# A message-passing and hash-expert kernel: 7,424 of its 8,192 edges sorted on the chip into runs of one source and one destination block

## What is computed

```
feat = concatenate([n_f[edge_src], n_f[edge_dst]], axis=1)   # 8192 edges
e_hh = relu(feat[:128]    @ W_hh + b_hh)     # edge tile 0
e_oo = relu(feat[128:768] @ W_oo + b_oo)     # edge tiles 1 to 5
e_ho = relu(feat[768:]    @ W_ho + b_ho)     # edge tiles 6 to 63: the "ho" edges
logit = ([e_hh, e_oo, e_ho] @ W_a + b_a)[:, 0]
ex    = exp(logit - segment_max(logit, edge_dst)[edge_dst])
alpha = ex / segment_sum(ex, edge_dst)[edge_dst]
z_f   = segment_sum(alpha[:, None] * n_f[edge_src], edge_dst)
h_new, o_new = relu([n_f, z_f][:64] @ W_hn + b_hn), relu([n_f, z_f][64:] @ W_on + b_on)
```

## Time and profile before

| | us |
|---|---|
| median of 3 runs | 871.84 (870.72 to 873.1) |
| the profiled execution's own time | 873.71 |
| its span, first to last instruction | 872.1 |
| TensorE busy | 807.4 (93%) |
| VectorE busy | 553.9 (64%) |
| ScalarE busy | 380.8 (44%) |
| GpSimd busy | 122.9 (14%) |

### The profile page before, as it was taken

One profiled execution on the slowest core, in us unless ns is written; L12 is line 12 of the kernel. 1 busy time (PEld: TensorE's weight loads), 2 busy tenths in 40 slices (PEclk: granted clock), 3 DMA queues, 4 the chain that ended last, 5 costly groups with the idle time before them and its releaser, 6 DMA issues.

```text
span 872.1 us, 10861 instructions
## 1 busy us (share of the span) xinstructions
PE 807.4 (93%) x3565; PEld 648.3 (74%) x3566; DVE 553.9 (64%) x822; ACT 380.8 (44%) x512; POOL 122.9 (14%) x143
## 2 busy tenths in 40 slices
PE   4899999979999969569997899999999999999998
PEld 4677788758888857457784578888888888888886
DVE  6874565559998899997645674445555544554443
ACT  3673454337665628154242343333444443344330
POOL 3010010012221336990003200000000000000000
PEclk9899999989999988888897989999999999999999
DMA  8676325312322220302255055555544554445521
GB/s 302 233 285 242 124 49 228 145 38 48 61 48 55 54 97 1 128 1 97 96 193 194 0 193 192 192 192 192 167 159 165 183 186 165 162 168 185 192 97 48
DMA packets 49600, 121.18 MB, mean 139 GB/s; under 512 B 2613, under 2 KB 35765, under 8 KB 47018
## 3 DMA queue, kind: packets, MB, share of 16 engines
q1 hardware_dynamic: 46122, 112.39, 36.0%
q0 software_dynamic: 2976, 8.13, 4.3%
q10 hardware_dynamic: 480, 0.36, 0.2%
HBM read 119.82 MB, written 1.05 MB: 139 GB/s over the span
## 4 chain that ended last, share of the span: by engine, by line
PE 84%; DVE 9%; issue 5%; ACT 1%; DMA 1%; DVEq 1%; POOL 0%; SPq 0%; ACTq 0%
PE ps L1013 19%; PE ps L1015 19%; PE ps L1014 19%; PE ps L1035 13%; PE ps L1042 5%; PE ps L1202 4%; PE ps L983 2%; DVE junk L850 2%; PE ps L1240 1%; PE ps L1257 1%; PE ps L1004 1%; DVE route L938 1%; DVE wlo L674 1%; DMA xt<-in_x_dram 1%; DVE oh_dst L872 1%
## 5 line engine op out<-in xcount | busy, mean ns | idle before, releaser
L674 DVE TENSOR_TENSOR wlo<-raw,whi 128x2048 fp32r<-128x2048 f32 x95 | 215.0, 2288 | 84.9 <-ACT whi L468 84.9
L468 ACT ACTIVATE whi<-raw 128x2048 fp32r<-128x2048 f32 x104 | 195.7, 1910 | 114.9 <-PE ps L1015 99.3
L1013 PE MATMUL ps<-whi,nT_hi 128*128 128x512 f32 x432 | 175.9, 407 | 1.7 <-POOL wlo L413 1.7
L1014 PE MATMUL ps<-whi,nT_lo 128*128 128x512 f32 x432 | 173.2, 401 | 0.0
L1015 PE MATMUL ps<-wlo,nT_hi 128*128 128x512 f32 x432 | 173.0, 400 | 0.0
L1035 PE MATMUL ps<-tab_hi,onehot 128*128 128x512 f32 x252 | 101.1, 401 | 12.3 <-issue 6.4
L1035 PE MATMUL ps<-tab_lo,onehot 128*128 128x512 f32 x252 | 100.3, 398 | 0.0
L1013 PEld LDWEIGHTS ps<-whi,nT_hi 128*128 128x128 f32 x432 | 82.6, 191 | 23.1 <-POOL wlo L413 2.1
L1015 PEld LDWEIGHTS ps<-wlo,nT_hi 128*128 128x128 f32 x432 | 82.8, 192 | 20.3
L1014 PEld LDWEIGHTS ps<-whi,nT_lo 128*128 128x128 f32 x432 | 82.9, 192 | 19.2
L946 DVE TENSOR_TENSOR gw<-act_g,route 128x512 f32<-128x512 f32 x32 | 20.7, 688 | 119.1 <-ACT act_g L635 119.1
(11 more groups left out here) (169 smaller groups left out, 988.1 us busy)
## 6 DMA issues: line engine op xcount, KB each, us to landing
raw<-n_L_ffn_values_down_dram SPq DMA_DIRECT2D x16, 2048.0 KB, 8.3
raw<-in_L_ffn_values_up_dram SPq DMA_DIRECT2D x16, 2048.0 KB, 7.5
raw<-in_L_gnn_W_hh_dram SPq DMA_DIRECT2D x4, 2048.0 KB, 10.2
raw<-in_L_gnn_W_oo_dram SPq DMA_DIRECT2D x4, 2048.0 KB, 7.8
raw<-in_L_gnn_W_ho_dram SPq DMA_DIRECT2D x4, 2048.0 KB, 7.8
raw<-in_L_gnn_W_hn_dram SPq DMA_DIRECT2D x4, 2048.0 KB, 7.4
raw<-in_L_gnn_W_on_dram SPq DMA_DIRECT2D x4, 2048.0 KB, 7.4
idx_b<-in_src_dram POOLq DMA_DIRECT2D x31, 128.0 KB, 3.2
```

The source lines that it names most:

```text
L468: nc.scalar.activation(half(whi, s, j, down), half(raw, s, j, down), ACT.Copy)\
L674: nc.vector.tensor_tensor(half(wlo, s, j, down), half(raw, s, j, down), half(whi, s, j, down).bitcast(F32), ALU.subtract)\
L1013: nc.tensor.matmul(o, a_hi, b_hi, start=start, stop=False)
L1014: nc.tensor.matmul(o, a_lo, b_hi, start=False, stop=False)
```

## The change

The first six tiles (`HEAD`) stay as tiles. The 58 ho tiles are sorted. VectorE computes for every ho edge its bucket, 4 x destination block + source block, one of 16. TensorE counts and ranks the edges (`count_buckets`, `rank_edges`), VectorE turns ranks into slots (`places`), each bucket padded to a multiple of 128, and lists each window's two blocks (`window_rows`). A window is 128 slots of one bucket; 58 tiles and at most 16 paddings make 74 windows, always. The node numbers are moved to their slots by 58 one-hot matmuls, in 15 chunks of up to four (`permute`), whose rows GpSimd and whose columns VectorE makes (`chunk_row`, `chunk_columns`); the matmuls stand among those of the head tiles and of `project(2, 0)`. `decode` copies the result.

Both tables are now stacked by block. TensorE spreads the indices of two windows over the partitions (`spread`, four matmuls of 128 x 128), ScalarE makes the one-hots from them in two instructions of 512 columns (`ring`), and a window takes four matmuls of 128 x 512, whose table blocks come from two registers read with `value_load`. A head tile takes 16 matmuls as before; VectorE makes its eight one-hots. VectorE's `dot` writes into PSUM; `window_peak` updates 64 columns of `segmax` at a place read with a `value_load`. GpSimd makes three tiles of 64 columns per window ahead of that (`same`, `oh_src`, `pen`). The maximum pass has 80 columns instead of 64, with the `lo` work of units 14 and 15 in it, which GpSimd did. In the sums, a window takes one `value_load` and two matmuls of 64 x 64; `oh_dst` is made for 18 or 19 windows at a time. The loops over windows are unrolled, and three pairs of PSUM banks take windows in turn. Nothing in the experts' part changes.

```diff
+HEAD = 6
+FIRST_TILE = [0, 1, HEAD]
+JT = ET - HEAD
+NBK = 16
+WN = JT + NBK
+COLS = HEAD + WN
+CHUNK = 4
+CHUNKS = (JT + CHUNK - 1) // CHUNK
...
+            pool.wait_ge(sorted_ready, 1)
+            for n in range(CHUNKS):
+                if n >= 2:
+                    pool.wait_ge(permuted, n - 1)
+                for j in range(CHUNK * n, min(CHUNK * n + CHUNK, JT)):
+                    last = nc.gpsimd.tensor_scalar(chunk_row[:, n % 2, j % CHUNK, :], iota16[:, 0:P], keep[:, 3, j:j + 1],
+                                                   None, ALU.is_equal)
+                last.then_inc(row_ready, 1)
+
...
+            pool.wait_ge(decoded, 1)
+            pool.wait_ge(gathered, HEAD)
+            for w in range(WN):
+                nc.gpsimd.tensor_scalar(same[:, w % 2, :], iota16[:, 1:NH + 1], slot_idx[:, 1, w:w + 1], None,
+                                        ALU.is_equal).then_inc(win_same, 1)
+                nc.gpsimd.tensor_scalar(oh_src[:, w, :], iota16[:, 1:NH + 1], slot_idx[:, 0, w:w + 1], None,
+                                        ALU.is_equal).then_inc(win_src, 1)
+                pool.wait_ge(win_same, w + 1)
+                nc.gpsimd.tensor_scalar(pen[:, w, :], same[:, w % 2, :], 1.0, -NEVER,
+                                        ALU.subtract, ALU.mult).then_inc(win_pen, 1)
...
+            for i in range(WN // 2):
+                act.wait_ge(bcast_done, i + 1)
+                if i:
+                    act.wait_ge(onehot_ready, i)
+                else:
+                    act.wait_ge(seg_done, HEAD)
+                nc.scalar.activation(gap, bank(i % 2), ACT.Abs, bias=rel_neg[:, 0:1]).then_inc(gap_ready, 1)
+                act.wait_ge(gap_ready, i + 1)
+                if i >= 2:
+                    act.wait_ge(gathered, HEAD + 2 * i - 2)
+                nc.scalar.activation(ring[:, i % 2, :, :].rearrange("p n e -> p (n e)"), gap, ACT.Relu,
+                                     bias=1.0, scale=-1.0).then_inc(onehot_ready, 1)
...
+            def head_onehot(i):
+
+                dve.wait_ge(batch_loaded, 32)
+                if i >= 3:
+                    dve.wait_ge(gathered, i - 1)
+                for a in range(2):
+                    for b in range(4):
+                        last = nc.vector.tensor_scalar(ohx[:, i % 2, 4 * a + b, :], idx_b[:, a, i * P:(i + 1) * P],
+                                                       block_pos[:, b:b + 1], None, ALU.is_equal)
+                last.then_inc(head_ready, 1)
...
+            def places():
+
+                dve.wait_ge(ranked, 1)
...
+                link(last)
+                link(nc.vector.tensor_tensor(place[:], place[:], in_bucket[:], ALU.mult))
+                link(nc.vector.tensor_reduce(slot[:], place[:].rearrange("p k j -> p j k"), mybir.AxisListType.X, ALU.add))
+                link(nc.vector.tensor_copy(slot_i[:, 0, :], slot[:]))
+                nc.vector.tensor_scalar(slot_i[:, 1, :], slot_i[:, 0, :], 7, None, ALU.arith_shift_right)
+                link(nc.vector.tensor_scalar(slot_i[:, 2, :], slot_i[:, 0, :], P - 1, None, ALU.bitwise_and))
+                nc.vector.tensor_copy(keep[:, 2:4, :], slot_i[:, 1:3, :]).then_inc(sorted_ready, 1)
...
+            def window_rows():
+
+                begun = place[:].rearrange("p k j -> p (k j)")
+                for first in range(0, WN, WN // 2):
...
+            def chunk_columns(n):
+
+                dve.wait_ge(sorted_ready, 1)
+                if n >= 2:
+                    dve.wait_ge(permuted, n - 1)
+                for j in range(CHUNK * n, min(CHUNK * n + CHUNK, JT)):
+                    for a in range(2):
+                        last = nc.vector.tensor_scalar(chunk_col[:, n % 2, j % CHUNK, a * WN:(a + 1) * WN],
+                                                       iota16[:, 0:WN], keep[:, 2, j:j + 1], keep[:, a, j:j + 1],
+                                                       ALU.is_equal, ALU.mult)
+                last.then_inc(col_ready, 1)
+
...
-                        loop_onehot(it, j // 2)
-            for i in range(ET - 4, ET):
+            places()
+            chunk_columns(0)
+            chunk_columns(1)
+            window_rows()
+            lo(1, 2)
+            lo(0, 3)
+            table_lo(1, 0)
+            lo(1, 3)
+            lo(0, 4)
+            table_lo(1, 1)
+            for i in range(1, HEAD):
                 edge_tile(i, pair_of(i))
-            dve.wait_ge(seg_done, ET)
+                if i + 2 < HEAD:
+                    head_onehot(i + 2)
+                chunk_columns(i + 1)
+            lo(1, 4)
+            for n in range(HEAD + 1, HEAD + 5):
+                chunk_columns(n)
+            lo(0, 5)
+            for n in range(HEAD + 5, CHUNKS):
+                chunk_columns(n)
+            decode()
+            table_lo(2, 0)
...
+            def dot(i, q):
+                dve.wait_ge(gathered, i + 1)
+                nc.vector.scalar_tensor_tensor(out=bank(q, 2), in0=bank(q, 2), scalar=0.0, in1=wa_b[:],
+                                               op0=ALU.max, op1=ALU.mult,
+                                               accum_out=logit[:, i:i + 1]).then_inc(dot_done, 1)
...
+            def window_peak(w):
+                base = dve.value_load(win_row[0:1, 2, w:w + 1], min_val=0, max_val=3 * NH)
+                dve.wait_ge(win_pen, w + 1)
+                dve.wait_ge(dot_done, HEAD + w + 1)
+                dve.wait_ge(seg_done, HEAD + w)
+                some = segmax[:, bass.ds(base, NH)]
+                nc.vector.scalar_tensor_tensor(out=some, in0=pen[:, w, :], scalar=logit[:, HEAD + w:HEAD + w + 1],
+                                               in1=some, op0=ALU.add, op1=ALU.max).then_inc(seg_done, 1)
+
+            dve.wait_ge(windows_ready, 1)
+            for w in range(WN):
+                dot(HEAD + w, 2 + 2 * (w % 3))
+                if w == 24:
+                    lo(1, 6)
+                if w:
+                    window_peak(w - 1)
...
+            for first, last, unit in ((1, COLS // 8, 0), (COLS // 8, COLS // 4, 1)):
+                with dve.Fori(first, last) as i:
+                    for s in range(4):
+                        dve.wait_ge(peak_done, 4 * i - 3 + s)
+                        edge_peak(4 * i + s, s)
+                lo(unit, 7)
...
+                    for n in range(PARTS):
+                        some = slice(n * WN // PARTS, (n + 1) * WN // PARTS)
+                        cols = slice(HEAD + some.start, HEAD + some.stop)
+                        for part, e in enumerate((ex_hi, ex_lo)):
+                            last = nc.vector.scalar_tensor_tensor(
+                                out=oh_dst[:, part, some, :], in0=pen[:, some, :], scalar=0.0,
+                                in1=e[:, cols].unsqueeze(2).to_broadcast([P, some.stop - some.start, NH]),
+                                op0=ALU.is_equal, op1=ALU.mult)
+                        last.then_inc(oh_ready, 1)
...
+            def gather(q, a, b, src_at, dst_at):
+
+                for h in range(2):
+                    for n, at in enumerate(src_at):
+                        nc.tensor.matmul(bank(q + h), a[n], src_rows[:, at[h]], start=n == 0, stop=False)
+                    for n, at in enumerate(dst_at):
+                        last = nc.tensor.matmul(bank(q + h), b[n], dst_rows[:, at[h]], start=False,
+                                                stop=n == len(dst_at) - 1)
                 last.then_inc(gathered, 1)
...
+            def spread(i):
+
+                if i >= 2:
+                    pe.wait_ge(gap_ready, i - 1)
+                for n in range(4):
+                    w, a = 2 * i + n // 2, n % 2
+                    last = nc.tensor.matmul(bank(i % 2)[:, n * P:(n + 1) * P],
+                                            slot_idx16[:, a, w:w + 1].to_broadcast([P, P]), ident16[:],
+                                            start=True, stop=True)
+                last.then_inc(bcast_done, 1)
...
+            def between(k, h, c):
+
+                if k == 1 and h == 0 and c == 1:
+                    count_buckets()
+                if k == 1 and h == 0 and c == 3:
+                    rank_edges()
+                if k == 2 and h == 0:
+                    permute(HEAD - 1 + c)
+                if k == 2 and h == 1 and c == C // 2 - 1:
+                    pe.wait_ge(tablo_ready, 12)
+                    pe.wait_ge(decoded, 1)
+                    spread(0)
+                    spread(1)
 
...
+            for i in range(WN // 2):
+                if i + 2 < WN // 2:
+                    spread(i + 2)
+                pe.wait_ge(onehot_ready, i + 1)
+                for w in (2 * i, 2 * i + 1):
+                    a = pe.value_load(win_row[0:1, 0, w:w + 1], min_val=0, max_val=3 * D)
+                    b = pe.value_load(win_row[0:1, 1, w:w + 1], min_val=0, max_val=3 * D)
+                    if w >= 3:
+                        pe.wait_ge(dot_done, HEAD + w - 2)
```

(19 more changed lines are left out.)

613 lines of the change are left out of this document (293 added, 320 removed).

## The result

| | before | after |
|---|---|---|
| median, us | 871.28 (869.88 to 873.1, 4 runs) | 932.24 (930.62 to 934.73, 4 runs) |
| ratio after / before | | 1.070, 95% interval 1.067 to 1.073 |
| the profiled execution's own time, us | 873.71 | 934.73 |
| its span, us | 872.1 | 933.0 |

A forecast was written before the change was run, and what follows sets the result against it. TensorE bounds most stages, VectorE the maximum pass; after the change TensorE's sequencer, through address reads, bounds the windows. Terms 37.9 - 15.0 + 0.8 + 24.0 + 2 = +49.7 us give 922 us, 5.7% slower, range 885 to 950.

The forecast's parts named there:

- The read: Window stage: each TensorE address read costs 0.64 us, two a window; windows 1.9 us apart, stage 142.1 us, -15.0.
- (c): Windows: TensorE slowed by half clock or waits for one-hots to 2.4 us a window, 959 us; chance 0.14.
- (a): Windows and summing: reads cost almost nothing, VectorE sets the windows at 1.5 us, 867 us, faster; chance 0.05.
- (b): Reads hide in the windows but not in the summing: -44.6 in place of -15.0, 892 us; chance 0.15.
- The summing: Summing stage: nothing covers the read, 0.78 us a window, 62.3 us against 38.3, +24.0.
- copies and a lower clock, +2: After the summing's tiny matmuls: `pT` copies in four pieces and a lower clock, +2, between 0 and 5.
- The standstill: Sort ahead of `project(1, 0)`'s c = 4: TensorE idle 20.5 us behind VectorE's sort work; shift +24.0, half clock after it +2.4.
- The head tiles: Head tiles before the windows: VectorE needs 5.1 us a tile against TensorE's 3.9, tiles 4 and 5 wait, +3.5.
- `project(2, 0)`, the step that failed: In `project(2, 0)`: eight permutes (2.4 us), more VectorE work, last chunks alternating with TensorE, then `decode`; +7.
- the second step that failed: Between `project(2, 0)` and the first window: only two spreads and their waits charged, +1.
- The maximum pass: Maximum pass: 80 columns and two `lo` on VectorE, GpSimd's work removed; 48.6 us against 47.8, +0.8.
- (d): First projection: the sort leaves no standstill, VectorE's part done beside the projection, 899 us; chance 0.06.

The follow-up runs named there:

- experiment 1: The changed kernel with constants in place of TensorE's two address reads per window in the window stage; 898.7 us.
- experiment 3: The changed kernel with a constant in place of TensorE's one read per window in the summing; 883.3 us.
- experiment 4: The changed kernel with VectorE's list reordered, `lo` splits ahead of the sort's placing and window rows; 920.1 us.
- experiment 5: The changed kernel with the bounds check of all address reads left out, loads kept; 880.0 us, 1.009 of the kernel before.
- experiment 6: The changed kernel with one unchecked load bringing the addresses of four windows, on TensorE and VectorE; 858.4 us, 0.984 of the kernel before.
- experiment 2: The changed kernel with a third TensorE read per window in the window stage, same result; 977.0 us.

## Why the prediction was right, and where it was off

The forecast case occurred: slower, by the sequencer in the windows and in the summing, with a standstill for the sort. 932.2 against 922 is 10.2 us too few, and nearly all of it lies before the first window (10.7 by stages). The window stage, forecast 3.0 us too long, hides a part of what the other stages missed. Step by step:

- **The read.** 0.64 us was taken from one read of three steps. A third read costs 0.62, and the windows came 1.86 us apart on average and 1.82 in the timeline, against a sum of 1.81 and the 1.9 that I took. The stage with its tail was 139.1 us, not 142.1; of the 0.1 for imperfect overlap half was needed. A load alone takes 0.297 to 0.300 us (medians of 74 at each line). The 0.14 of (c) had a higher price of the read within it; no run shows one.
- **VectorE behind it.** I gave it 1.5 us a window. Without reads the stage was 107.9 us with 4.6 of `lo` in it, so (107.9 - 4.6 - 1.5) / 74 = 1.38. Rivals (a) and (b) had 112.5 us for the stage; 107.9 were measured, and with the 4.6 of `lo` inside, which they had left out although nothing covers it at VectorE's pace. Had reads been free, the kernel would have been faster than before: 932.2 less 33.6 and 49.0 is 850 us (an estimate from experiments 1 and 3).
- **GpSimd.** Mis-sized, without effect on the time: its three instructions took 0.50, 0.50 and 0.49 us on average, 1.5 a window and not 1.1. They started at 184.2 us and stayed ahead of the windows at 1.86, and by their early start even in experiment 1, where the windows came faster than they did.
- **The summing.** 0.78 us a window, as worked out, and 25.9 for the stage against 24.0. Most of the difference is the clock, granted at 0.57 in the stage; the last 32 head matmuls took 5.2 us in the chain, where they took 3.6 at full clock in experiment 3. I had put this into another term, "copies and a lower clock, +2".
- **The standstill.** Forecast 20.5 us. The chain of waits shows its parts: `places` from 66.34 to 75.36, so 9.0 as forecast; 16 columns of 4.3 instead of 3.9; `window_rows` 5.4 instead of 5.3; the half split 2.3. Sum 21.0, and TensorE's wait is 21.1. Experiment 4 shows that this wait was the order of VectorE's list.

```profile
66.34 0.19 DVE total L753
...
75.36 4.30 DVE chunk_col L811 x16
79.67 0.66 DVE place L784
...
85.08 2.30 DVE wlo L648
87.43 0.79 PE ps L1095
```

- **The head tiles.** They began at 130.7 us, 26.6 later than before; forecast 26.4. They took 19.5 us to the first permute of `project(2, 0)` instead of 15.3, so 4.2 against 3.5.
- **`project(2, 0)`, the step that failed.** From 150.2 to 184.3 us, against 119.4 to 141.2 before: +12.3, where +7 was forecast. The eight permutes cost about what was said (0.28 to 0.32 us each at full clock). The waits were undersized: I had counted the work of VectorE and its turns with TensorE at the end, but not GpSimd's rows (0.78 us each on average, three waits of 2.2 in all), nor the wait for the columns of chunk 7 behind a split, nor the clock, 0.95 in this stage against 1.00 in the kernel before. TensorE's waits in it are 2.8 for columns, 2.2 for rows, and 1.6 for `decode`:

```profile
PE ps L1156 <- DVE chunk_col L811: 2.8, 1, 2.8
PE ps L1156 <- POOL chunk_row L452: 2.2, 3, 1.1
...
PE ps L1102 <- DVE dst_col L826: 1.6, 1, 1.6
```

- **Behind it, the second step that failed.** `project(2, 1)`, the spreads and their waits took 33.1 us instead of 27.6: +5.5, where only +1 for the spreads was forecast. Two things had been put at nothing. The first is the clock: TensorE was granted 0.50 from 185.8 to 192.4 us, and 0.88 over the whole stretch against 1.00 before, which costs at most 0.12 x 33.1 = 4 us (an estimate). The second is the end of the stretch. TensorE's last matmul of the projection began at 211.65; then it waited for VectorE's last split of the destination table and for the first two reads:

```profile
PE ps L1166 <- DVE tab_dst L853: 3.6, 1, 3.6
...
PE ps L1112 <- issue: 1.4, 1, 1.4
```

Before, the first 14 matmuls of edge tile 6 stood in front of that split, from 165.04 us on, and TensorE waited for 0.4 us. I had charged one fall of the clock, after the long standstill. The clock of this stretch fell 1.5 us after a wait of 1.6, so a long standstill is not needed for it; in experiment 4 it even was 0.83 from 80 to 90 us, in which, as from 50 us on, TensorE was busy without a gap. What makes it fall there is not shown.

- **The maximum pass.** +3.0 instead of +0.8. While GpSimd made its six `head_src` tiles, six of VectorE's instructions took 0.61 to 0.73 us start to start instead of 0.41 (1.4 us, as in the earlier trace rows). And behind the first half of the `lo` of unit 15 TensorE had 24 matmuls of that unit to do before the first pair. They began at 398.33, 0.43 us apart, at a clock of 0.50 until 404 us (0.23 apart behind it, at 0.99), the first pair came at 407.3, and the sum had left them out:

```profile
398.33 0.80 PE L1095 MATMUL ps<-whi,nT_hi 128*128 128x512 f32 x1 [6.72 <-DVE wlo L648]
398.93 0.63 PE L1096 MATMUL ps<-whi,nT_lo 128*128 128x512 f32 x1
399.36 0.63 PE L1097 MATMUL ps<-wlo,nT_hi 128*128 128x512 f32 x1
```

- **Rivals.** (a) and (b) are what experiments 5 and 6 built: they fall where a read costs as much as it does here, and hold once it doesn't. (c) did not occur: the clock was 0.98 in the windows, so many short idle times of 0.6 us did not bring it down there, with TensorE busy for 99.2 of 139.1 us. In the summing TensorE was busy for 30.0 of 64.2 us, and the clock was 0.57. How near (c) was, experiment 2 shows: with one more read per window the clock of the stage was 0.82. (d) was put to the test by experiment 4. Another order of VectorE's list does remove the standstill, but saves 12 us by the medians, not 22.

What is left open: how the 12.3 us of `project(2, 0)` divide between clock and waits was read from one trace and not tried apart.

## What to carry to other kernels

A read of a dynamic address takes time in the instruction list of the engine that needs it, here 0.62 us with its check. Set that against the work that the same engine does per address; if the reads and register steps are more, the list is the bound (here 1.81 us a window by the sum and 1.86 measured, against VectorE's 1.38). Before giving up on dynamic addresses, load several with one instruction and drop the check where the value is bounded by construction: here that alone turned 7.0% slower into 1.6% faster, and 2.9% faster together with the reordering of experiment 4. New work on a side engine goes behind what the main engine waits for next: here that order alone gave 12.1 us. And a forecast should leave room for stretches at half clock, behind short waits too (here 0.50 from 185.8 to 192.4 us, 1.5 us behind a wait of 1.6).

## What the runs showed that I had not expected

- Four values in one load took 0.331 us against 0.298 for one, which is 0.083 us a value.
- The check of a read cost 0.29 us, as much as its load, though its two steps show 0.17.
- Kernels 1, 2, 3, 5 and 6 do the same work up to the first window as the changed kernel, but for the form of a few loads, and the first gather came at 211.0, 213.7, 217.3, 213.6 and 212.4 us there, and at 217.4 in the changed kernel. The granted clock differs: from 87.4 to 101 us it was 0.89, 0.87, 0.78, 0.88 and 0.86 in them, and 0.78 in the changed kernel; the two at 0.78 are the two that came last. So 4 to 6 us of the 10.7 that the forecast missed ahead of the first window may be of this kind. That is argued and not shown, since each kernel has one profile, and the four executions of the changed kernel lie within 4.1 us. The total times carry it too: one of the four executions of kernel 3 took 877.8 us at a mean clock of 0.955, the others 883.1 to 883.4 at 0.944 to 0.948.

```profile
87.40:101.00 13.60, 13.57 (x47) 10.98 (x48) 6.58 (x3) 0.90 (x1) 0.00 (x0) 0.78 0.78 306
```

```profile
87.40:101.00 13.60, 13.60 (x53) 10.89 (x54) 7.80 (x5) 2.38 (x3) 0.00 (x0) 0.89 0.77 306
```

The first row is of the changed kernel, the second of kernel 1: 47 matmuls started in the same 13.6 us in one, 53 in the other.
- A chain of waits can follow an engine that holds up nobody. In kernel 1 it named GpSimd for 75% of the window stage, with VectorE idle for 0.7 us before 72 dots. An engine's own idle time is the better witness.
